# Two shared tiles whose second half runs behind the last routed tile, and a last read-back in eight transfers

## What is computed

```
def _L1_ffn_ref(x, gate_w, w1, w2, w3, sw1, sw2, sw3):
    def _swiglu(x, wa, wb, wo):
        return jax.nn.silu(x @ wa.T) * (x @ wb.T) @ wo.T
    xf = x.reshape(-1, x.shape[-1])                  # 1024 x 256
    probs = jax.nn.softmax(xf @ gate_w.T, axis=-1)   # 15 routed experts
    weights, indices = jax.lax.top_k(probs, 2)
    combine = zeros((T, 15)).at[arange(T)[:, None], indices].add(weights)
    y = zeros_like(xf)
    for i in range(15):
        y = y + _swiglu(xf, w1[i], w3[i], w2[i]) * combine[:, i:i + 1]   # inner width 176
    z = _swiglu(xf, sw1, sw3, sw2)                                       # shared, inner width 176
    return (y + z).reshape(shape)

x = x + tanh(g_xattn[0]) * _L0_xattn_ref(_layernorm(x), ctx_512, ...)
x = x + tanh(g_ffn[0])   * _L0_ffn_ref(_layernorm(x), ...)               # 8 experts, two per token
x = x + tanh(g_xattn[1]) * _L1_xattn_ref(ctx_512, _layernorm(x), ...)
x = x + tanh(g_ffn[1])   * _L1_ffn_ref(_layernorm(x), ...)
```

## Time and profile before

| what | value |
|---|---|
| median of 3 timed runs | 373.45 us (373.22, 373.45, 375.45) |
| time of the profiled execution | 371.48 us |
| its span | 369.7 us |
| mean granted TensorE clock | 0.897 |
| busy: PE, DVE, ACT, POOL | 320.5, 208.5, 148.9, 111.6 us |
| moved by DMA | 48.41 MB, mean 131 GB/s |

### The profile page before, as it was taken

The page is one execution under the profiler, slowest core; times in us unless marked ns, Lnnn a source line. Parts: engine busy times, 40 slices in busy tenths (PEclk is TensorE's granted clock), DMA queues, the critical chain, the costliest instruction groups (busy, mean ns, idle before and its releaser), DMA issues.

```text
span 369.7 us, 6926 instructions
## 1 busy us (share of the span) xinstructions
PE 320.5 (87%) x2144; PEld 184.2 (50%) x2144; DVE 208.5 (56%) x655; ACT 148.9 (40%) x315; POOL 111.6 (30%) x106
## 2 busy tenths in 40 slices
PE   8974599899999999999999999018868999999991
PEld 6643494456555555555555555008434444444440
DVE  1678874754544455555454453494764754555236
ACT  1565413134443433433444343156133455555540
POOL 0021141123243322222222111231043677773310
PEclk9995556999999999999999999755578999999997
DMA  7999919996937461635221111502021232331146
GB/s 233 346 311 317 294 41 291 287 293 176 222 56 227 125 179 32 200 79 132 31 37 14 21 25 15 128 20 97 0 58 30 78 94 89 97 90 57 45 147 225
DMA packets 21147, 48.41 MB, mean 131 GB/s; under 512 B 2600, under 2 KB 11688, under 8 KB 20088
## 3 DMA queue, kind: packets, MB, share of 16 engines
q1 hardware_dynamic: 14680, 35.78, 31.0%
q0 software_dynamic: 6048, 11.28, 13.8%
q10 hardware_dynamic: 384, 0.90, 0.8%
HBM read 37.98 MB, written 9.96 MB: 130 GB/s over the span
## 4 chain that ended last, share of the span: by engine, by line
PE 74%; DVE 13%; DMA 6%; issue 2%; ACT 2%; POOL 1%; SPq 0%; ACTq 0%; DVEq 0%; POOLq 0%
PE bank L1381 27%; PE bank L1355 21%; PE bank L1431 9%; PE bank L1345 6%; PE bank L1194 4%; PE bank L1254 3%; DMA wgu<-results 2%; DMA rows<-x 2%; DVE st L721 2%; DVE z L905 1%; DMA sums<-y_sb,route_dst 1%; DVE z L799 1%; PE bank L1323 1%; PE bank L1274 1%; PE bank L1202 1%
## 5 line engine op out<-in xcount | busy, mean ns | idle before, releaser
L1381 PE MATMUL bank<-wgu,xT 128*64 x320 | 99.2, 464 | 1.6 <-DVE xT L1005 0.9
L1381 PE MATMUL bank<-rows,xT 128*64 128x344 f32 x320 | 99.2, 464 | 0.0
L1355 PE MATMUL bank<-wdn,hT 120*64 (+2 forms) x396 | 89.1, 388 | 4.2 <-ACT hT L579 3.9
L1355 PEld LDWEIGHTS bank<-wdn,hT 120*64 120x64 f32 (+1 forms) x396 | 48.5, 139 | 44.0 <-issue 18.8
L1381 PEld LDWEIGHTS bank<-wgu,xT 128*64 128x64 f32 x320 | 43.0, 139 | 47.4 <-issue 7.9
L419 POOL DMA_INDIRECT sums<-y_sb,route_dst x20 | 31.7, 1585 | 115.4 <-ACT y_sb L617 97.5
L411 POOL DMA_INDIRECT x_in<-rows,route_tok x43 | 42.4, 985 | 57.6 <-DVE route_tok L911 29.0
L985 DVE SCALAR_TENSOR_TENSOR hh<-th,bank 128x344 f32<-128x344 f32 x40 | 20.5, 513 | 58.2 <-ACT th L568 58.2
L1355 PE MATMUL bank<-rows,hT 120*64 120x256 f32 x228 | 52.3, 379 | 0.0
L1381 PEld LDWEIGHTS bank<-rows,xT 128*64 128x64 f32 x320 | 43.1, 140 | 0.0
L568 ACT ACTIVATE th<-bank 128x344 f32<-128x344 f32 x40 | 18.3, 457 | 59.3 <-PE bank L1381 59.3
(11 more groups left out here) (160 smaller groups left out, 447.3 us busy)
## 6 DMA issues: line engine op xcount, KB each, us to landing
wgu<-gu SPq DMA_DIRECT2D x8, 1376.0 KB, 18.8
wdn<-wd SPq DMA_DIRECT2D x8, 720.0 KB, 22.2
wgu<-gu SPq DMA_DIRECT2D x3, 1408.0 KB, 6.6
wdn<-wd SPq DMA_DIRECT2D x5, 576.0 KB, 8.6
rows<-rows SPq DMA_DIRECT2D x8, 256.0 KB, 3.5
wgu<-results SPq DMA_DIRECT2D x4, 512.0 KB, 5.9
wgu<-gu SPq DMA_DIRECT2D x1, 1056.0 KB, 7.8
rows<-xt SPq DMA_DIRECT2D x4, 256.0 KB, 7.8
```

The lines of the kernel that those rows point to most:

```text
L1355: last = mm(psum[7][part, 0:H], hT[0:m.wide, j * P:(j + 1) * P][:, part], wd(j), start=(j == 0), stop=(j == m.chunks - 1))
L1381: last = mm(psum[2 * c + g][part, 0:CH0], xT[:, r, k * P:(k + 1) * P][:, part], w, start=(k == 0), stop=(k == KH - 1))
```

## The change

1. Turn and down of shared tiles 2 and 3 move: they no longer run between the first routed tiles but behind the last routed tile, ahead of shared tiles 4 to 7 (`last1`). Gate, up, tanh and product of 2 and 3 stay early. Their products go to a new buffer `kept_h` in the spare part of `wgu`, whose 2 x 16 unused columns are zeroed once; so products 2 and 3 wait for no turn.
2. ScalarE copies hT and z of shared tile 1 before it waits for the routing's owners; before it waited for them behind tile 0. Its `copy_hT` and `copy_z` of tiles 2 and 3 move to the end.
3. The routed tiles take the places of the done counters right behind shared tile 1 (AHEAD = 2 in place of NS = 4).
4. The seven semaphores `w1_here[n]` become one with the total count: one wait per engine in place of seven.
5. The last read-back is made in eight transfers of one token tile (256 KB) in place of four of 512 KB, and `combine(m, i)` works on one tile: first half, a wait for it, second half.
6. VectorE adds shared tiles 2 and 3 at the end too. Its list behind its last `hidden` is now: add 2, 3; combine 0, 1, 2, 3; add 4, 5; combine 4, 5; add 6, 7; combine 6, 7.

Cut to its core (renamings and declarations are left out):

```
+AHEAD = 2
+        kept = spare + 2 * GU1 + 2 * WD1
+        kept_h = wgu[:, kept:kept + (NS - AHEAD) * NF1 * FC1].rearrange("p (i f) -> p i f", f=NF1 * FC1)
...
@@ sync @@
-                    for b in range(B):
-                        sp.dma_start(y_got[:, 2 * b:2 * b + 2, :, :].rearrange("p i k h -> p i (k h)"),
-                                     results_t[:, 2 * b:2 * b + 2, :]).then_inc(m.y_here[b], 16)
+                    for i in range(NT):
+                        sp.dma_start(y_got[:, i, :, :].rearrange("p k h -> p (k h)"),
+                                     results_t[:, i, :]).then_inc(m.y_here[i], 16)
...
@@ scalar @@
-            for n, (_, gu_a, gu_z, dn_a, dn_z) in enumerate(second_weights()):
-                act.wait_ge(w1_here[n], 16 * (gu_z > gu_a) + 16 * (dn_z > dn_a))
-            for i in range(NS):
+            act.wait_ge(w1_here, W1_ALL)
+            for i in range(AHEAD):
                 copy_hT(m1, i, i % 2)
-                if i >= NS - 2:
-                    tanh_half(m1, i + 2, i % 2)
                 copy_z(i, i)
-                if i == 0:
-                    act.wait_ge(m1.experts_ready, 1)
-                if i < 2:
-                    stage_down1(i)
+            act.wait_ge(m1.experts_ready, 1)
+            stage_down1(0)
+            tanh_half(m1, NS, 0)
+            stage_down1(1)
+            tanh_half(m1, NS + 1, 1)
...
+            def last1(i):
+                copy_hT(m1, m1.S + i, i % 2)
+                if NS <= i < NT - 2:
+                    tanh_half(m1, m1.S + i + 2, (m1.S + i) % 2)
+                copy_z(i, m1.S + i)
...
@@ vector @@
-                    since(dve, m.hT_done, t - 1)
+                    since(dve, m.hT_done, t - (NS - AHEAD + 1) if t < NS + m.S + 2 else t - 1)
...
-                since(dve, m1.hT_done, i - 1)
-                nc.vector.scalar_tensor_tensor(out=hh1[:, i % 2, 0:F1], in0=th_early[:, i, :], scalar=1.0,
+                product = hh1[:, i, 0:F1] if i < AHEAD else kept_h[:, i - AHEAD, 0:F1]
+                nc.vector.scalar_tensor_tensor(out=product, in0=th_early[:, i, :], scalar=1.0,
...
@@ tensor @@
-            for i in range(2):
-                turn_h(m1, i, i)
+            for i in range(AHEAD):
+                turn_h(m1, i, hh1[:, i, :])
                 since(pe, z_copied, i)
                 down_shared(i)
             pe.wait_ge(m1.experts_ready, 1)
             for i in range(2):
                 turn_x(m1, i, i)
-                turn_h(m1, i + 2, i)
                 gate_up_slots(i, i)
-                since(pe, z_copied, i + 2)
-                down_shared(i + 2)
...
+            def last1(i):
+                if i < NS:
+                    turn_h(m1, i, kept_h[:, i - AHEAD, :])
                 else:
+                    turn_h(m1, m1.S + i, hh1[:, (m1.S + i) % 2, :])
+                if NS <= i < NT - 2:
+                    gate_up_shared((m1.S + i) % 2, xnT[:, i + 2, :])
+                if i == AHEAD:
+                    pe.wait_ge(m1.y_copied, m1.S)
+                pe.wait_ge(z_copied, i)
+                down_shared(m1.S + i)
+            steps(step1, m1.S)
+            for i in range(AHEAD, NT):
+                last1(i)
```

More of the change, by code:

```diff
@@ L185, in build @@
         w0_order, first_staged, ends_ready = sem("w0_order"), sem("first_staged"), sem("ends_ready")
-        w1_here = [sem(f"w1_here{i}") for i, _ in enumerate(second_weights())]
+        w1_here = sem("w1_here")
+        W1_ALL = 16 * sum((gu_z > gu_a) + (dn_z > dn_a) for _, gu_a, gu_z, dn_a, dn_z in second_weights())
         out_stored = sem("out_stored")
@@ L215, in work @@
         def work(name, *shape, dt=fp32):
-            if name not in kept:
+            if name not in homes:
                 most = LARGEST.get(name, S1)
                 if name == "scmp":
-                    kept[name] = lower[:, 0:most]
+                    homes[name] = lower[:, 0:most]
                 elif name in STAY:
-                    kept[name] = sb("route_" + name, [P, most], dt)
+                    homes[name] = sb("route_" + name, [P, most], dt)
                 else:
@@ L262, in __init__ @@
                 m.hT_done = sem(f"hT_done{n}")
-                m.hT_copied_a, m.hT_copied_v = sem(f"hT_copied_a{n}"), sem(f"hT_copied_v{n}")
+                m.hT_copied_a = sem(f"hT_copied_a{n}")
+                if n == 0:
+                    m.hT_copied_v = sem("hT_copied_v")
                 m.y_done, m.y_copied = sem(f"y_done{n}"), sem(f"y_copied{n}")
                 m.y_stored = [sem(f"y_stored{n}{r}") for r in range(RING if n else 0)]
-                m.y_here = [sem(f"y_here{n}{b}") for b in range(B)]
-                m.x_new = sem(f"x_new{n}")
+                m.y_here = [sem(f"y_here{n}{b}") for b in range(NT if n else B)]
+                if n == 1:
+                    m.x_new = sem("x_new")
                 m.half = sem(f"half{n}")
@@ L1063, in _, with combine @@
             steps(step0, m.S)
-            def combine(m, b):
-                dve.wait_ge(m.y_here[b], 16)
-                ends = [did(nc.vector.scalar_tensor_tensor(
+            def combine(m, i):
+                dve.wait_ge(m.y_here[i], 16)
+                then(nc.vector.scalar_tensor_tensor(
                     out=xs[:, i, :], in0=y_got[:, i, 0, :], scalar=m.c1[:, i:i + 1], in1=xs[:, i, :],
-                    op0=ALU.mult, op1=ALU.add)) for i in (2 * b, 2 * b + 1)]
-                for i, end in zip((2 * b, 2 * b + 1), ends):
-                    after(end)
-                    nc.vector.scalar_tensor_tensor(
-                        out=xs[:, i, :], in0=y_got[:, i, 1, :], scalar=m.c2[:, i:i + 1], in1=xs[:, i, :],
-                        op0=ALU.mult, op1=ALU.add).then_inc(m.x_new, 1)
+                    op0=ALU.mult, op1=ALU.add))
+                nc.vector.scalar_tensor_tensor(
+                    out=xs[:, i, :], in0=y_got[:, i, 1, :], scalar=m.c2[:, i:i + 1], in1=xs[:, i, :],
+                    op0=ALU.mult, op1=ALU.add).then_inc(m.x_new, 1)
             m1 = mix[1]
@@ L1118, in _ @@
             norm_terms(B - 1, m1.rstd, m1.terms)
+            nc.vector.memset(kept_h[:, :, F1:NF1 * FC1], 0.0)
             def hidden_early(i):
@@ L1174, in add_late @@
                 nc.vector.tensor_tensor(xs[:, i, :], edge[:, i, :], xs[:, i, :], ALU.add).then_inc(late_added, 1)
-            dve.wait_ge(z_added, NS)
+            dve.wait_ge(z_added, AHEAD)
+            for i in range(AHEAD, NS):
+                add_late(i)
+            dve.wait_ge(late_added, NS - AHEAD)
+            for i in range(NS):
+                combine(m1, i)
             add_late(NS)
             add_late(NS + 1)
-            combine(m1, 0)
+            dve.wait_ge(late_added, NS + 2 - AHEAD)
+            combine(m1, NS)
+            combine(m1, NS + 1)
             add_late(NS + 2)
-            combine(m1, 1)
             add_late(NS + 3)
-            dve.wait_ge(late_added, NT - NS)
-            combine(m1, 2)
-            combine(m1, 3)
+            dve.wait_ge(late_added, NT - AHEAD)
+            combine(m1, NS + 2)
+            combine(m1, NS + 3)
         @block.tensor
@@ L1456, in _ @@
             ranks(m1)
[L1457 to L1458 removed]
+            pe.wait_ge(w1_here, W1_ALL)
             for i in range(NS):
@@ L1491, in step1 @@
                     gate_up_slots(s + 2, r % 2)
[L1492 removed]
+                else:
                     gate_up_shared(r % 2, xnT[:, NS + s + 2 - m1.S, :])
                 if s == 0:
[L1495 to L1506 removed]
+                    pe.wait_ge(z_copied, AHEAD)
+                since(pe, m1.y_copied, s)
+                at = owner(m1, s) * WD1 + WD1
+                pe.wait_ge(m1.dn_staged, s + 1)
+                down(m1, s + AHEAD, lambda j: wdn[0:FC1, bass.ds(at + j * H, H)],
+                     lambda j: stage_dn1[0:FC1, s % 2, j * H:(j + 1) * H])
+            def last1(i):
+                if i < NS:
+                    turn_h(m1, i, kept_h[:, i - AHEAD, :])
+                else:
+                    turn_h(m1, m1.S + i, hh1[:, (m1.S + i) % 2, :])
[6 more added lines that the diff above has]
+            steps(step1, m1.S)
+            for i in range(AHEAD, NT):
+                last1(i)
 def _constants():
```

61 lines of the change are left out of this document (21 added, 40 removed).

## The result

| | before | after |
|---|---|---|
| median of 20 runs each | 374.93 us | 375.61 us |
| lowest to highest | 372.97 to 375.99 | 374.31 to 379.79 |
| ratio after/before, 95% interval | | 1.0043 [1.0022, 1.0064] |
| profiled execution, its span | 371.48, 369.7 | 377.33, 375.4 |

The change costs a little: 0.4%, 1.6 us by the ratio (the two medians alone differ by 0.7). That is within 1%, and inside the range, but 1.0 us above the number forecast. The two profiled spans lie much further apart, 5.7 us, and that is where the lesson of this case is.

The account below looks back on a forecast made before the run. TensorE, 74% of the chain, was taken as the bound, except at the last mixture's head and the end. End 4.3 us minus head 3.2 gave +1.1 on 373.45: 374.6 us, range 371.8 to 376.5.

Parts of the forecast that it names:

- The end: Behind the last routed tile: VectorE's list behind a later product 7 bounds; the end moves by 4.3 us minus the head's gain.
- The dependent halves: Combines at the end: the second half waits for the first, 0.91 us a tile where 0.80 was paid.
- The head: Start of the last mixture: earlier hT copy and moved downs and turns let routed tiles end 3.2 us earlier.
- its three cases: Clock at the head: back at 280.0, G 3.2 us; full or back sooner, 4.4 to 5.3 (chance 0.25); low longer, 2.0 (0.14).
- G: How much earlier the routed tiles end, read at the third xT copy: 285.10 - 281.87 = 3.2 us.
- The likeliest case: Head of the last mixture: clock back at full level at 280.0, G = 3.2 us; forecast chance 0.45.
- The pace: Routed tiles between head and end: same instructions as before, so 2.93 us a step kept.
- the base: Whole kernel: median of three timed runs before, 373.45 us, moved by 1.1 us to give 374.6.
- The read-back rival: End of the kernel: the end follows the read-back, VectorE's list is no bound; gain 4.8 us, 368.7 us; chance 0.05.
- the free second half: Combines at the end: the second half's wait costs nothing, 0.80 us a tile; 0.9 us less, 373.7 us; chance 0.05.
- a pace other than 2.93: Routed steps: listed sign that the prediction is wrong, as it would shift G and the result by 4.3 - G.

Follow-up runs that it names:

- kept tiles last: Changed kernel with shared tiles finished 4, 5, 6, 7, 2, 3, read-back and store following, combines in pairs, adds of 2 and 3 last: 372.81 us, ratio 0.9929.
- its second profile: The kernel before, unchanged, timed and profiled once more: 376.03 us, ratio 1.0007, span 373.5.
- the owner load: Kernel before, with TensorE reading a routed tile's owner once, for its gate, and keeping it for the down: 374.79 us, ratio 0.9977.
- the staging copy: Kernel before, with VectorE copying only 4 of 704 columns of staged gate and up weights from routed tile 4 on: 374.89 us, ratio 0.9978.
- a later gather: GpSimd's gather of tile s + 7 held until tile s's down is done: kernel before 376.50 us, ratio 1.0014; version finishing kept tiles last 373.46 us, 0.9943.

## Why the prediction was right and wrong

**The end: right in its mechanism, its size too small.** Product 7 moved from 5.42 us behind the turn that follows the last routed tile to 9.42 (363.56 - 354.14): the +4.0 of two steps of 2.01. No combine waited for a transfer; SP started 3.33 us behind that turn, as before. The list took 9.71 us against 9.83 forecast, with 0.92 or 0.93 a combine. The other side of that term was mis-sized: before's own list, 9.49 in the profile, was 8.82 in the second one and about that in five of eight. The end therefore costs 4.9 us as a rule, not 4.3. Another 0.3 us, the last routed step but one at 3.22, the sum had put at nothing; why it is longer was not looked into. The trace shows its down waiting for ScalarE's hT copy.

**The dependent halves: right.** A second half starts 0.52 us behind the first, an independent one 0.41 (364.26, 364.78, 365.19). The Trainium skill, "VectorE: DVE Perf Modes", section "The DRAIN you can't avoid", found no extra cost for a semaphore behind each of eight copies. For these combines the rows show one, 0.11 us for each dependent half.

**The head: right for one of its three cases.** The down of shared tile 1 came 0.41 us behind z (forecast 0.5); the first gate started 3.33 us behind the cast, before 5.10: 1.8 earlier (forecast 2). G was 3.1 where the clock was low for 6.8 us (forecast 3.2). But the clock took each of the forms named: low for 10.2 us in the profile after (G = 1.8, forecast 2.0 for it), never low with kept tiles last (G = 5.4, forecast 4.4 to 5.3). All five profiles with this head gave 14.2, 12.9, 12.9, 10.6 and 12.9 us from cast to first y. The likeliest case came three times in five. The Trainium skill, "TensorE: Matmul & The Clock Gate", section "HAM oscillation — how this bites in real kernels", has gaps in the matmul stream bring the clock down; the trace agrees only in part: the same code met all three, and in the one that stayed low longer TensorE was busy for 9.06 of 10.3 us, where it was busy for 5.83 of 6.9 in the shorter one.

**The pace and the base: wrong.** Two steps failed, and the second is the one that moved the number. "Behind this point each step has the same instructions as before, so I keep 2.93 us a step": the instructions are the same, the step was 3.16. Since before has the slow steps too (69.7 us in its second profile, 68.7 and 68.5 after), they all but cancel in the difference. And "The three timed runs have the median 373.45, 2 us higher; moved by the same 1.1 they give 374.6": that base was low by 1.5 us. 20 runs gave 374.93, and the four later sessions 374.94, 375.72, 376.19 and 375.62; so the forecast of a slower kernel, 374.6, lies below the kernel that it started from. The one profiled execution of before, 371.48 us, lay below the lowest timed run of every session (372.47), and I had noted it was 2 us under the median without asking what in its trace was untypical. It lacked the slow steps, 4 to 6 us. Moved from 374.93 instead, the forecast 1.1 gives 376.0, against 375.61 and 375.86 measured. In the difference, the forecast 4.3 - 3.2 = +1.1 us is inside both intervals ([0.8, 2.4] and [0.0, 2.1] us); with the measured sizes it is 4.9 + 0.3 - 3.1 = +2.1, inside the first and at the upper edge of the second. Direction and rough size were right; that 1.1 fits no worse than 2.1 is owed to the width of the intervals and proves no term.

**The rivals.** The read-back rival and the free second half fall to the rows above. Of a rival in which the pace itself varies the prediction had nothing; "a pace other than 2.93" stood only among the signs.

**Open.** Why an indirect gather delays the release of ScalarE by TensorE's results was not found; neither the owner load nor the staging copy nor a later gather decided it, and whether it is the gather's kind or the length of its issue is not shown. Whether matmuls end late there or only their signal comes late, the trace can't say, since their ends are modelled. Nor is it known why one execution of twelve had none.

## What to carry to other kernels

Work moved off a busy stretch must be put where nobody stands behind it: the end became 4.9 us longer when the two tiles ran ahead of the last gates, and 0.3 to 1.0 us (14.4 and 15.1 against 14.1) when they ran last and VectorE's list was put in order with them, which turned the ratio from 1.0043 to 0.9929. Before a sum is built on a profile, hold its own time against the spread of the timed runs, and take it as one draw: a periodic step time can have two forms in the same program. Three timed runs are a thin base for a forecast to a microsecond. A split transfer is worth something only where its consumer waits for it.

## What the runs showed of the hardware

- With an indirect gather and an indirect scatter issued by GpSimd in each step, about every other step of the routed loop took 3.4 to 3.9 us in place of 2.93 in eleven of twelve profiles, 4 to 6 us in all over the 22 steps. With plain transfers in the gathers' place, from SyncE or from GpSimd, 64.5 and 64.1 us for what took 68 to 70. I had expected GpSimd's issue to be hidden, being off the chain.
- The issue of a gather measures 0.97 us, that of a plain transfer of the same size on the same queue 0.58. A scatter's issue measures 0.97 to 1.00 us, and about 1.18 when it starts while VectorE copies within SBUF (18 in the first profile of before at 1.14 to 1.33, though three in its second stay at 0.99; with the copy at 4 columns none start so).
- With the same code at the head, TensorE's clock stayed at 2.4 GHz there in one execution, was at 1.2 GHz for 6.8 us in three, and for 10.2 us in one; the two profiles of the changed kernel itself had 10.2 and 6.8.
